# Joining two linear maps of a graph network's node update into one, and running it by group inside the loop that closes the edge sums

## The reference

```python
edge_input = concatenate([x[src], edge_attr], axis=-1)
messages = gelu(edge_input @ mW1 + mb1) @ mW2 + mb2
gates = sigmoid(gelu(edge_input @ gW1 + gb1) @ gW2 + gb2)
aggregated = segment_sum(messages * gates, dst)
combined = concatenate([x, aggregated], axis=-1)
update = gelu(combined @ uW1 + ub1) @ uW2 + ub2
h = x + update            # then a layer norm, and the next layer
```

## Time and profile before

| | us |
|---|---|
| median of three runs | 6146.88 (6139.91 to 6166.58) |
| profiled execution | 6141.51 |
| its span | 6139.7 |
| TensorE busy | 4875.2 (79%) |
| VectorE busy | 3676.9 (60%) |
| GpSimd busy | 2863.9 (47%) |
| ScalarE busy | 2481.1 (40%) |

### The profile page before, as it was taken

One profiled execution on the slowest core, in us unless ns is written; L12 is line 12 of the kernel. 1 busy time (PEld: TensorE's weight loads), 2 busy tenths in 40 slices (PEclk: granted clock), 3 DMA queues, 4 the chain that ended last, 5 costly groups with the idle time before them and its releaser, 6 DMA issues.

```text
span 6139.7 us, 94960 instructions
## 1 busy us (share of the span) xinstructions
PE 4875.2 (79%) x32966; PEld 2860.3 (47%) x32966; DVE 3676.9 (60%) x6227; ACT 2481.1 (40%) x4310; POOL 2863.9 (47%) x3038
## 2 busy tenths in 40 slices
PE   4888999999999665565655555555479999999999
PEld 3777777777777432332323333333343333333334
DVE  7999623242332544444444444444379999999998
ACT  5777300010000222232322332322157777777777
POOL 3000000000000466666666666666327777777777
PEclk6999999989999777777777777777689999999999
DMA  2333587858778343433334343434111111111111
GB/s 63 147 150 153 190 268 221 268 165 268 245 241 251 97 120 117 119 115 119 114 119 120 115 119 115 121 113 121 28 31 56 50 56 51 51 57 51 56 50 33
DMA packets 296196, 759.03 MB, mean 124 GB/s; under 512 B 81000, under 2 KB 183464, under 8 KB 289704
## 3 DMA queue, kind: packets, MB, share of 16 engines
q1 hardware_dynamic: 217352, 595.36, 30.0%
q0 software_dynamic: 78624, 160.79, 9.9%
HBM read 589.77 MB, written 166.22 MB: 123 GB/s over the span
## 4 chain that ended last, share of the span: by engine, by line
PE 54%; another core or an unknown queue 19%; DVE 11%; issue 9%; ACT 4%; DVEq 1%; POOL 1%; DMA 0%; ACTq 0%; SPq 0%; POOLq 0%
PE p_e L1020 19%; PE p_e L1144 12%; PE p_tr L1157 9%; PE p_mm L1128 3%; PE p_e L1052 2%; PE p_e L1058 2%; ACT GA L1362 1%; PE p_mm L984 1%; PE p_tr L1052 1%; ACT L1362 1%; ACT L1353 1%; DVE VA L1645 1%; DVE GA L1645 1%; DVE R L1645 1%
## 5 line engine op out<-in xcount | busy, mean ns | idle before, releaser
L719 POOL DMA_INDIRECT GA<-table_mg,VA x1568 | 1485.8, 948 | 2167.4 <-DMA table_mg<-VA 1389.0
L2048 DVE TENSOR_TENSOR VA<-VA,p_mm 128x1024 f32<-128x1024 f32 (+1 forms) x1274 | 1417.9, 1155 | 137.3 <-POOL VA L818 122.8
L818 POOL TENSOR_SCALAR VA<-VA 128x1024 f32<-128x1024 f32 (+1 forms) x1274 | 1243.3, 995 | 430.3 <-ACT VA L1413 426.2
L1052 PE MATMUL p_e<-BD,EA 128*128 128x384 f32 x896 | 397.3, 596 | 531.5 <-ACT GA L1362 497.4
L1413 ACT ACTIVATE VA<-p_e 128x1024 f32<-128x1024 f32 (+1 forms) x637 | 621.7, 976 | 355.8 <-PE p_e L1144 355.8
L1890 DVE SCALAR_TENSOR_TENSOR R<-R,kp,M 128x97 f32<-128x97 f32 x1568 | 512.6, 327 | 345.2 <-issue 252.5
L1157 PE MATMUL p_tr<-VA,GA 128*32 128x512 f32 (+1 forms) x5096 | 648.3, 581 | 0.4 <-DVE VA L2048 0.2
L1863 DVE TENSOR_TENSOR M<-GA,p_mm 128x1344 f32<-128x1344 f32 x112 | 174.0, 1554 | 751.7 <-ACT GA L1362 736.5
L1020 PE MATMUL p_e<-GA,VA 128*128 128x288 bf16 x4802 | 608.4, 287 | 0.0
L1020 PE MATMUL p_e<-GA 128*128 128x288 bf16 x4802 | 607.7, 287 | 0.0
L1058 PE MATMUL p_e<-GA,C 128*128 128x384 f32 x896 | 427.1, 635 | 222.7 <-DMA GA<-table_mg,VA 222.4
(11 more groups left out here) (226 smaller groups left out, 7228.2 us busy)
## 6 DMA issues: line engine op xcount, KB each, us to landing
GA<-adj SPq DMA_DIRECT2D x98, 800.0 KB, 4.7
VA<-adj SPq DMA_DIRECT2D x98, 800.0 KB, 4.7
run_m<-R SPq DMA_DIRECT2D x112, 700.0 KB
GA<-adj SPq DMA_DIRECT2D x98, 768.0 KB, 4.5
VA<-adj SPq DMA_DIRECT2D x98, 768.0 KB, 4.5
H<-adj SPq DMA_DIRECT2D x56, 896.0 KB, 5.1
adj<-GA SPq DMA_DIRECT2D x25, 1568.0 KB, 5.2
adj<-VA SPq DMA_DIRECT2D x24, 1568.0 KB, 5.2
```

What stands on the lines that cost most here:

```text
L719: pool.indirect_dma_start(out=to, out_offset=None, in_=of, in_offset=bass.IndirectOffsetOnAxis(ap=at, axis=0)).then_inc(s, 16)
L818: pool.tensor_scalar(e, e, HIGH, LOW, ALU.min, ALU.max).then_inc(clipped, 1)
L1052: mm = pe.matmul(p_h[k][0:CH, 0:4 * D], EA[:, h, k // 2, :], BD[:, 2 * (k % 2):2 * (k % 2) + 2, :, :].rearrange("p a b f -> p (a b f)"), s ...
L2048: dve.tensor_tensor(e, e, p_mm[n % 2][:, 0:across(b)].unsqueeze(1).to_broadcast([P, 2, across(b)]), ALU.mult).then_inc(weighed, 1)
```

## The change

The two linear maps mW2 and uW1_a have nothing between them, so that S @ mW2 @ uW1_a + s * (mb2 @ uW1_a) = [S, s] @ J, with J of 97 rows and 96 columns. `join_weights` makes J on the chip between the two-weight layer and the uW1_x layer: TensorE turns mW2 and mb2 (two transposes), ScalarE copies both to hT, TensorE multiplies by uW1_a, and VectorE copies the product to `W_sums`, the place of mW2 in W, made one row longer. hT also gets more partitions.

The loop of step 3 then also does the update, each group two steps behind: TensorE turns the 97 sums of the group before (`turn_sums`), ScalarE copies them, TensorE multiplies the group before that by J (`update`), VectorE adds it to T, and ScalarE takes Gelu of that group. The uW2 layer waits for the Gelu of each group (`gelu_nodes`) instead of for all of them. The product of the gate sums with mb2, both separate layers and the whole-array Gelu are gone on this way, and `gelu_wanted` is given at the end of the loop. `open_nodes` loses a wait.

```diff
-FAST_STAGES = 8 + 3 * GROUPS + 1
+FAST_STAGES = 5 + 3 * GROUPS + 1
-        W = sb("W", [D, len(WEIGHTS), D])
+        W_all = sb("W", [P, len(WEIGHTS), D])
+        W = W_all[0:D, :, :]
+        W_sums = W_all[0:MW, WEIGHTS.index("L2_gnn_mW2"), :]
-        hT = sb("hT", [D, 2, GRP * P])
+        hT_sums = sb("hT", [P, 2, GRP * P])
+        hT = hT_sums[0:D, :, :]
...
 # TensorE
+            def join_weights():
+                k = at["turn"]
+                wait(pe, hT_ready, k - 1)
+                pe.transpose(p_tr[k % 2][0:D, 0:D], W[:, WEIGHTS.index("L2_gnn_mW2"), :], ident[0:D, 0:D])
+                pe.transpose(p_tr[k % 2][0:D, P:2 * P], B[:, BIASES.index("L2_gnn_mb2"), :], ident).then_inc(turned, 1)
+                pe.wait_ge(hT_ready, k + 1)
+                pe.wait_ge(product_used, at["mm"] - 1)
+                pe.matmul(p_mm[at["mm"] % 2][0:MW, 0:D], hT[:, k % 2, 0:MW], W[:, WEIGHTS.index("uW1_a"), :], start=True,
+                          stop=True).then_inc(product, 1)
+            def close_and_update():
+                closed = {}
+                def close(g):
+                    pe.wait_ge(open_ready, g + 1)
+                    pe.wait_ge(product_used, at["mm"] - 1)
...
+                    closed[g] = at["mm"]
+                def turn_sums(g):
+                    k = at["turn"] + g
+                    pe.wait_ge(product_used, closed[g])
+                    pe.wait_ge(hT_ready, k - 1)
+                    for t in tiles_of(g):
+                        o = (t - GRP * g) * P
+                        mm = pe.transpose(p_tr[k % 2][0:MW, o:o + P], AGG[:, t, 0:MW], ident)
+                    mm.then_inc(turned, 1)
+                def update(g):
+                    k = at["turn"] + g
+                    pe.wait_ge(hT_ready, k + 1)
+                    pe.wait_ge(product_used, at["mm"] - 1)
+                    for t in tiles_of(g):
+                        o = t - GRP * g
+                        mm = pe.matmul(p_mm[at["mm"] % 2][:, o * D:(o + 1) * D], hT_sums[0:MW, k % 2, o * P:(o + 1) * P],
+                                       W_sums, start=True, stop=True)
+                    mm.then_inc(product, 1)
+                    at["mm"] += 1
+                for g in range(GROUPS + 2):
+                    if g < GROUPS:
+                        close(g)
+                    if 1 <= g <= GROUPS:
+                        turn_sums(g - 1)
+                    if g >= 2:
+                        update(g - 2)
...
-                dense(AGG, ["L2_gnn_mW2"])
-                dense(V, ["uW1_a"])
-                dense(T, ["L2_gnn_uW2"])
+                    dense(AGG, ["L2_gnn_mW2"])
+                    dense(V, ["uW1_a"])
+                dense(T, ["L2_gnn_uW2"], behind_gelu=fast)
 # ScalarE
+            def update_nodes():
+                for g in range(GROUPS + 2):
...
+                    if 1 <= g <= GROUPS:
+                        k = at["turn"]
+                        act.wait_ge(turned, k + 1)
+                        act.activation(hT_sums[0:MW, k % 2, 0:across(g - 1)], p_tr[k % 2][0:MW, 0:across(g - 1)], ACT.Copy
+                                       ).then_inc(hT_ready, 1)
...
+                    if g >= 2:
+                        at["mm"] += 1
+                        group = slice(GRP * (g - 2), GRP * (g - 2) + len(tiles_of(g - 2)))
+                        act.wait_ge(product_used, at["mm"])
+                        act.activation(T[:, group, :], T[:, group, :], ACT.Gelu).then_inc(gelu_nodes, 1)
# VectorE
                 def open_nodes(g):
-                    if g >= 2:
-                        dve.wait_ge(product, at["mm"] - 1)
...
+                def update(g):
...
+                    dve.wait_ge(product, at["mm"] + 1)
+                    dve.tensor_tensor(to, p_mm[at["mm"] % 2][:, 0:n_t * D].rearrange("p (t f) -> p t f", t=n_t), to,
+                                      ALU.add).then_inc(product_used, 1)
+                for g in range(GROUPS + 2):
+                    if g + 1 < GROUPS:
+                        open_nodes(g + 1)
+                    if g < GROUPS:
+                        sum_ends(g)
+                    if g >= 2:
+                        update(g - 2)
...
+                    dve.wait_ge(product, at["mm"] + 1)
+                    dve.tensor_copy(W_sums, p_mm[at["mm"] % 2][0:MW, 0:D]).then_inc(product_used, 1)
...
                 if fast:
                     sum_pass()
+                    dve.sem_inc(gelu_wanted, 1)
```

## The result

| | median us | runs | ratio to before |
|---|---|---|---|
| kernel before | 6151.20 (6136.44 to 6169.08) | 20 | |
| changed kernel | 6137.44 (6107.62 to 6144.97) | 20 | 0.9978 [0.9969, 0.9987] |

A forecast was written before the change was run, and what follows sets the result against it. The prediction saw late TensorE signals during gathers, then a serial 48.4 us stretch. Gains of 22.9 (loop) and 5.6 (uW2 layer) less 0.3 (joining) made 28.2 us: 6118 from a median of 6146.88, range 6088 to 6147.

The forecast's parts named there:

- local sum: From the late signals' end through the uW2 layer: gains of 22.9 and 5.6 us; less 0.3 for joining weights, 28.2.
- 6113 in its terms: Whole time forecast on the profiled execution's scale: its 6141.51 us less the 28.2 us gain.
- late signals: During GpSimd's gather bursts, TensorE's finished products reach VectorE 27 to 30 us late; prompt once the gathers are over.
- Rival (2): Closing loop: no late signals, the records being one execution's accident; gain 55.3 us, time 6091; chance 0.09.
- Groups left: Closing loop: late signals come singly, so 8 of 13 groups are left when they end at 4402.
- rival (1): Closing loop: late signals come in bunches, leaving 5 groups at 4402; gain 35.4 us, time 6111; chance 0.18.
- The uW2 layer: Layer behind the closing loop: starts with TensorE busy and takes 18.6 us instead of 24.2.
- clock term of 5.6 us: uW2 layer: TensorE no longer idles during Gelu and falls to the lower clock; 18.6 us instead of 24.2.
- rival (3): Edge pass start: TensorE's work shifts against the first gathers, one more late signal, up to 21.2 us; 6140; chance 0.12.
- (5): Closing loop: the change hides nothing, all 13 groups run behind the gathers; gain 16 us, time 6131; chance 0.05.
- (4): Closing loop: late signals outlast the gathers, some 24 at 3.5 us add 84 us; time 6202; chance 0.06.

The follow-up runs named there:

- set 4: Runs made together on one chip, signals late: kernel before 6131.16 us, changed kernel unchanged 6105.12, and two variants with extra TensorE products in the last block, 6122.20 and 6102.95.
- sets 1 and 4: The two sets of runs, each made together on one chip, with signals late; kernel before 6136.46 and 6131.16 us.
- sets 2, 3 and 5: The three sets of runs, each made together on one chip, with no signals late (prompt); kernel before 5855.65, 5856.08 and 5856.07 us.
- before_warm: Kernel before plus extra unread TensorE products in the attention's last block, 3 in each of the first eight steps, 1 in the others: 6135.51 us against 6136.46.
- outside_warm: Changed kernel with extra last-block products in all steps, joined layer and Gelu by group moved to a second loop: 6107.08 us against 6104.29 inside the loop.
- before_start: Kernel before plus three extra unread TensorE products in each of the last attention block's first eight steps: 5853.54 us against 5856.08, prompt signals.
- after_start: Changed kernel plus three extra unread TensorE products in each of the last attention block's first eight steps: 5816.34 us; kernel before 5856.08, prompt signals.
- after_start_more: Repeat of after_start in a later set with prompt signals: 5818.88 us, changed kernel without the products 5837.00, kernel before 5856.07.
- landed_first: Changed kernel, but VectorE waits for all 49 gathers of edge sums before the closing loop: 6096.98 us in one run, kernel before 6136.46, late signals.
- the products in the first eight steps: Changed kernel plus three extra unread TensorE products in each of the last attention block's first eight steps: 5817.93, 5816.34 and 5818.88 us in three sets.
- the longer form of the products: Changed kernel plus extra TensorE products in all steps of the last attention block, 3 in the first eight, then 1: 6104.29 us against 6136.46 before.
- after_timed: Changed kernel, unchanged, run again with late signals: 6105.12 us against 6131.16 of the kernel before.
- after_again: Changed kernel, unchanged, run once more, with prompt signals: 5837.40 us in one run against 5855.65 of the kernel before.

## Why the prediction was wrong, point by point

- *What failed*: the step from the local sum to the whole time. "6113 in its terms" takes everything behind the uW2 layer as unmoved; the sum has no term for the attention, and gives no reason for that. The attention's last block is 53 or 76 us long, by TensorE's clock, and in the first measurement 19 of 20 executions of the changed kernel had, by their times, the long one. In the two traces: 28.4 us of local gain, plus 6.5 of an earlier loop, less 22.4 in the block and 1.0 behind it, which is 11.5, where the spans differ by 11.9. The 6.5 are of the size of the traces' scatter: with late signals the first gather of the edge pass came at 2030.7 to 2035.3 us in either kernel, and from it to the first end gather it took 2278 to 2298 us. Of the medians' 13.7 us, 28.4 less 22.4 leaves 6.0 explained; the other 8 are of the size of that scatter, and the kernel before has five runs from 6163 us on that may be its own long blocks, but no trace of them shows it. In set 4, where the block kept its clock, the unchanged kernel was 26.0 us [17.8 to 38.6 by the ratio's interval] faster than before, as forecast.
- *What could have warned*: the trace of before has TensorE busy for 46.6 of 46.6 us at 1.00 in that block, right behind an idle of 0.75 us. Its length hangs on the clock level, and the forecast had just priced such a fall in the uW2 layer.
- *Late signals*: as said. VectorE's idle before 4388.14 is 20.21 us again, "remote". Rival (2) took them for an accident of one execution's records; they are real in the first measurement and in sets 1 and 4, and in sets 2, 3 and 5 no VectorE wait of the loop is "remote".
- *Groups left*: 8 forecast, 8 measured, at the end of the late signals, which came 8 us after the last gather, as before. The count holds in all five traces with late signals and the update inside the loop; the three without it (before, before_warm, outside_warm) have 5 left. So rival (1), five left in the new loop, is out. Group times were 4.2 us at the lower level, as forecast, and 2.2 to 2.5 at the higher against 2.4. From 4395.92 to the first uW2 transposes, 4421.43: 25.5 us, the forecast's figure.
- *The uW2 layer*: 18.6 forecast, 18.7 measured, at 1.00. The clock term of 5.6 us is seen in the traces under late signals (18.7 us against 24.2), but no run there undid it alone. Under prompt ones it has the other sign: the statistics took 17.1 us in before_start and 20.6 in after_start, 24.0 in after_start_more.
- *Local sum*: from the end of the late signals to the end of the layer 72.6 us before, 44.2 after: 28.4, forecast 28.5.
- *Start of the pass*: rival (3) didn't come. TensorE's first edge products are at 2083.32 against 2085.83, within the 3 us named; the join isn't seen in the time.
- *Hides nothing / is slower*: (5) let all thirteen groups run behind the gathers, and eight did. Its price of 12 us for the other five didn't come: landed_first, which does run all thirteen there, took 37.7 us against 36.7, because its loop starts at the last landing and not at the end of the late signals. (4) is out: the first prompt signal came 8 us after the last gather.
- *Where luck came in*: the measured 6137 lies close to the times of (3), 6140, and (5), 6131, and inside the range, though neither mechanism ran. What put it there was the block that no rival names.
- *On the rule of the Trainium skill*: the prediction read "PE and ACT never wait on anyone" (page "SBUF — State Buffer", section "Who interferes with whom") as a loop without late products. The prompt sets agree with that reading, and the sets with late signals don't. The sentence is about ports of the on-chip memory, and in the rows TensorE itself ran its matmuls in time, so no run here shows it wrong.

The Trainium skill, page "TensorE: Matmul & The Clock Gate", section "Part 1: The HAM clock gate (the "warmup" mystery)", says that the point at which the clock changes differs from run to run of one kernel, since the monitor runs free of it. The two heaps of the kernel before and the sets of the changed one agree with that; why the share is one in three for one and nine in ten for the other was not settled.

What beats both kernels: the changed one with the products in the first eight steps, 37 to 40 us under before with prompt signals (ratios 0.9923, 0.9925, 0.9932), and with late ones, with the longer form of the products, 32 us (0.9953). They cost 2.9 us where the clock would have held.

## What to carry over

A sum for one stretch holds for that stretch: before adding it to the total, list the other places whose length has two values (here a narrow last block at either clock level, 22 us apart), because the same code drew one in one set of runs and the other in another. Guard such a place with cheap work at its start, or measure with the guard in both kernels to see the change alone. And what "inside the loop" is worth depends on how promptly the loop's signals come: here 3 us, within the scatter, with late ones, and 13 with prompt ones.

## What the runs showed of the hardware

Whether signals are late goes by set, not by kernel. GpSimd's gathers of the edge pass (groups by line; idle before by releaser) in the changed kernel with late signals (after_timed) and with prompt ones (after_again):

```profile
L722 POOL DMA_INDIRECT GA<-table_mg,VA x1568 | 1484.5, 947 | 2160.2 <-DMA table_mg<-VA 1389.0 <-issue 464.9 <-remote 279.7
```
```profile
L722 POOL DMA_INDIRECT GA<-table_mg,VA x1568 | 1492.4, 952 | 1891.5 <-DMA table_mg<-VA 1388.8 <-issue 502.7
```

The gathers themselves cost the same, 0.95 us each; the 280 us of "remote", 264 to 297 in all traces with late signals and none in the others, are about the difference of the two kinds, 4.6% of the time. Where that comes from no run here shows, nor whether the signal itself came late or the waiting engine took it late. Sets 2 and 3 (prompt) and set 4 (late) carry the same chip number in their results, so the chip alone, if that number names the same one each time, doesn't decide it. A narrow block can run at either clock level from its first few steps to its end, some 45 steps, on the same instructions: 53 us or 76. At the lower one TensorE was busy for all 69.0 us of the window by its records, and the clock stayed at 0.50.
